# The end of a fused attention and feed-forward kernel, tile by tile instead of stage by stage

## The reference

```python
x = L0_attn_Z_in
x = x + _layernorm(_L0_attn_ref(_layernorm(x), A_l, r_l, B_l, C_l))
x = x + _layernorm(_L0_ffn_ref(_layernorm(x), gate_w, up_w, down_w, gate_s, up_s, down_s))

# _L0_ffn_ref, for xf = x.reshape(b * s, h); h = 2048, inter = 5632
g = jnp.einsum('th,ih->ti', xf, gate_w) * gate_s
u = jnp.einsum('th,ih->ti', xf, up_w) * up_s
hdn = jax.nn.silu(g) * u
out = jnp.einsum('ti,hi->th', hdn, down_w) * down_s
```

## Time and profile before

| what | value |
|---|---|
| median of three runs | 1383.64 us (1381.90 to 1505.44) |
| the profiled execution's own time | 1382.18 us |
| its span on the slowest core, core 3 | 1380.6 us |
| spans of the eight cores | 1372.5 to 1380.6 us |
| granted TensorE clock, mean of each core | 0.928 to 0.930 |
| bytes moved by DMA on core 3 | 104.44 MB |

### The profile page before, as it was taken

The page is one execution under the profiler, slowest core; times in us unless marked ns, Lnnn a source line. Parts: engine busy times, 40 slices in busy tenths (PEclk is TensorE's granted clock), DMA queues, the critical chain, the costliest instruction groups (busy, mean ns, idle before and its releaser), DMA issues.

```text
span 1380.6 us, 12731 instructions; the slowest of 8 cores (1372.5 to 1380.6 us)
## 1 busy us (share of the span) xinstructions
PE 1142.6 (83%) x5236; PEld 505.5 (37%) x5236; DVE 350.3 (25%) x398; ACT 200.9 (15%) x255; POOL 53.7 (4%) x76
## 2 busy tenths in 40 slices
PE   2429889860799999999999999999999999999500
PEld 0103334320444444444444444444444444444200
DVE  2057344357310122101320113110131001312810
ACT  2402333243300000000000000000000000000242
POOL 1000000000000000000000000000000000000000
PEclk9959999985699999999999999999999999999755
DMA  6770000006993513844047440665307633030059
GB/s 116 204 161 1 1 1 0 1 24 240 160 156 63 90 32 47 136 87 88 10 70 127 86 84 1 89 125 92 61 1 116 122 68 61 0 61 0 0 92 151
DMA packets 27592, 104.44 MB, mean 76 GB/s; under 512 B 2320, under 2 KB 4880, under 8 KB 24080
## 3 DMA queue, kind: packets, MB, share of 16 engines
q0 software_dynamic: 23936, 83.63, 36.3%
q1 hardware_dynamic: 2448, 16.81, 3.3%
q10 hardware_dynamic: 1152, 3.20, 0.9%
HBM read 162.09 MB, written 16.78 MB: 130 GB/s over the span
## 4 chain that ended last, share of the span: by engine, by line
PE 66%; DMA 2%; DVE 2%; ACT 1%; issue 1%; POOLq 0%; DVEq 0%; ACTq 0%
PE ps_f L739 22%; PE ps_f L791 22%; PE ps_f L755 22%; DMA y<-w2b 2%; DVE acc L815 1%; ACT w2b L849 1%; DVE hdn L769 1%; DVE acc L804 0%; ACT w2b L820 0%; ACT L833 0%; POOLq L77 0%; DVEq L88 0%; ACT rW L835 0%; ACT tstat L833 0%; ACTq L88 0%
## 5 line engine op out<-in xcount | busy, mean ns | idle before, releaser
L739 PE MATMUL ps_f<-lnfT,gw_sb 128*128 128x512 bf16 x1408 | 313.4, 381 | 5.3 <-PEq L77 5.3
L791 PE MATMUL ps_f<-dwb,hdn 128*128 128x512 bf16 x1408 | 304.9, 379 | 11.4 <-DVE hdn L769 11.4
L755 PE MATMUL ps_f<-lnfT,uw_sb 128*128 128x512 bf16 x1408 | 311.1, 379 | 0.0
L791 PEld LDWEIGHTS ps_f<-dwb,hdn 128*128 128x128 bf16 x1408 | 137.4, 98 | 178.9 <-issue 14.1
L739 PEld LDWEIGHTS ps_f<-lnfT,gw_sb 128*128 128x128 bf16 x1408 | 138.3, 98 | 173.2 <-issue 8.7
L755 PEld LDWEIGHTS ps_f<-lnfT,uw_sb 128*128 128x128 bf16 x1408 | 137.7, 98 | 166.2
L769 DVE SCALAR_TENSOR_TENSOR hdn<-ps_f,us_sb,sg 128x1024 bf16<-128x1024 f32 x44 | 56.5, 1284 | 555.3 <-PE ps_f L755 555.3
L765 ACT ACTIVATE sg<-ps_f,gs_sb 128x1024 bf16<-128x1024 f32 x44 | 49.0, 1114 | 831.3 <-PE ps_f L739 831.3
L426 PE MATMUL ps_t<-att,xTb 128*128 128x512 bf16 x512 | 116.0, 384 | 37.7 <-DMA xTb<-xT 37.7
L804 DVE TENSOR_TENSOR acc<-acc,ps_f 128x2048 f32<-128x2048 f32 x40 | 91.5, 2288 | 172.1 <-PE ps_f L791 172.1
L426 PEld LDWEIGHTS ps_t<-att,xTb 128*128 128x128 bf16 x512 | 49.9, 99 | 100.6 <-issue 43.2
(11 more groups left out here) (103 smaller groups left out, 343.5 us busy)
## 6 DMA issues: line engine op xcount, KB each, us to landing
gw_sb<-gw POOLq DMA_DIRECT2D x22, 1024.0 KB, 8.3
uw_sb<-uw POOLq DMA_DIRECT2D x22, 1024.0 KB, 8.7
dwb<-dw POOLq DMA_DIRECT2D x11, 2048.0 KB, 19.4
xbuf<-x SPq DMA_DIRECT2D x8, 1024.0 KB, 22.6
y<-xbuf SPq DMA_DIRECT2D x8, 1024.0 KB, 4.0
y<-w2b POOLq DMA_DIRECT2D x8, 1024.0 KB, 10.1
xTb<-xT POOLq DMA_DIRECT2D x4, 1024.0 KB, 45.0
xtop_sb<-xtop ACTq DMA_DIRECT2D x2, 1024.0 KB, 9.9
```

The costliest lines, as they stand in the source:

```text
L739: e.matmul(ps_f[:, half, :], gw_sb[:, slot, ht * P:(ht + 1) * P], lnfT[:, ht, half * 512:(half + 1) * 512], start=(ht == 0), stop=(ht == H ...
L755: e.matmul(ps_f[:, 2 + half, :], uw_sb[:, slot, ht * P:(ht + 1) * P], lnfT[:, ht, half * 512:(half + 1) * 512], start=(ht == 0), stop=(ht ...
L791: e.matmul(ps_f[:, bs + hc, :], hdn[:, li, tt * P:(tt + 1) * P], dwb[:, li, hc * 512:(hc + 1) * 512], start=(li == 0), stop=(li == blk - 1)),
```

## The change

The three stages at the end become a function, emit_finale(tt), that is called for each tile of the last group right behind the tile's add. So the end is done tile by tile, in the order DSEQ, in between the down-projection adds. The statistics are computed on one column per tile (t1c, t2c, with rW8[:, 0:1] as scratch), and Ln writes lnt. The Square of a tile now waits for the store of tile tt - 2, since it writes the same buffer of w2b; Identity no longer needs to. What is computed, and the eight stores, stay as they were. The second wait of SP behind the last block was never emitted and is gone.

```diff
+    out_dma = {}
+
+    def emit_finale(tt):
+        pl.vop(lambda e, tt=tt: e.scalar_tensor_tensor(
+            acc[:, tt, :], acc[:, tt, :], 1.0, dsB[:, :], ALU.mult, ALU.mult,
+            accum_out=wsum[:, tt:tt + 1]),
+            w=[("sDV", accadd[(len(BLKS) - 1, tt)])])
+        w1v = pl.v("sDV")
+        pl.aop(lambda e, tt=tt: e.activation(
+            w2b[:, tt % 2, :], acc[:, tt, :], AF.Square,
+            accum_out=wsq[:, tt:tt + 1]),
+            w=[("sDV", w1v)] + ([out_dma[tt - 2]] if tt - 2 in out_dma
+                                else []))
+        sqv = pl.v("sAC")
+        pl.vop(lambda e, tt=tt: e.tensor_scalar(
+            t1c[:, :], wsum[:, tt:tt + 1], 1.0 / D, None, ALU.mult),
+            w=[("sAC", sqv)])
+        pl.vop(lambda e, tt=tt: e.tensor_scalar(
+            t2c[:, :], wsq[:, tt:tt + 1], 1.0 / D, None, ALU.mult))
+        pl.vop(lambda e: e.tensor_tensor(rW8[:, 0:1], t1c[:, :], t1c[:, :],
+                                         ALU.mult))
+        pl.vop(lambda e: e.tensor_tensor(t2c[:, :], t2c[:, :], rW8[:, 0:1],
+                                         ALU.subtract))
+        vst = pl.v("sDV")
+        pl.aop(lambda e, tt=tt: e.activation(
+            lnt[:, tt:tt + 1], t2c[:, :], AF.Ln, bias=c_eps),
+            w=[("sDV", vst)])
+        pl.aop(lambda e, tt=tt: e.activation(
+            rW8[:, tt:tt + 1], lnt[:, tt:tt + 1], AF.Exp, scale=c_nh))
+        rwv = pl.v("sAC")
+        pl.vop(lambda e, tt=tt: e.tensor_tensor(
+            ngW8[:, tt:tt + 1], t1c[:, :], rW8[:, tt:tt + 1], ALU.mult),
+            w=[("sAC", rwv)])
...
+        ngv = pl.v("sDV")
+        pl.aop(lambda e, tt=tt: e.activation(
+            w2b[:, tt % 2, :], acc[:, tt, :], AF.Identity,
+            scale=rW8[:, tt:tt + 1], bias=ngW8[:, tt:tt + 1]),
+            w=[("sDV", ngv)])
+        w2v = pl.v("sAC")
+        osem = "sOUT" if tt % 2 == 0 else "sRL"
+        pl.dma(osem, "gpsimd", t_y.ap()[tt * P:(tt + 1) * P, :],
+               w2b[:, tt % 2, :], w=[("sAC", w2v), ("sSP", SP)], accum=True)
+        out_dma[tt] = (osem, pl.v(osem))
...
             accadd[(bi, tt)] = pl.v("sDV")
+            if bi == len(BLKS) - 1:
+                emit_finale(tt)
```

More of the change, by code:

```diff
@@ L707, in build_nc @@
     dn_prev = {0: None, 4: None}
+    out_dma = {}
[30 more added lines that the diff above has]
+            w=[("sAC", rwv)])
+        pl.vop(lambda e, tt=tt: e.tensor_scalar_mul(
+            ngW8[:, tt:tt + 1], ngW8[:, tt:tt + 1], -1.0))
+        pl.vop(lambda e, tt=tt: e.tensor_tensor(
+            ngW8[:, tt:tt + 1], ngW8[:, tt:tt + 1], ngN8[:, tt:tt + 1],
+            ALU.add))
+        ngv = pl.v("sDV")
[8 more added lines that the diff above has]
+        out_dma[tt] = (osem, pl.v(osem))
@@ L809, in build_nc @@
             accadd[(bi, tt)] = pl.v("sDV")
[L811 to L855, removed]
@@ L856, in build_nc @@
-    pl.em("sync", fn=None, w=[out_dma[-1], out_dma[-2]])
+            if bi == len(BLKS) - 1:
+                emit_finale(tt)
+    pl.em("sync", fn=None, w=[out_dma[6], out_dma[7]])
     pl.emit(nc, sems)
@@ L861, in build_nc @@
     sTl.close()
-    pl.em("sync", fn=None, w=[("sOUT", out_dma[-1])])
     s2.close()
```

## The result

| | before | changed |
|---|---|---|
| median | 1382.48 us (1381.05 at lowest, 10 runs) | 1364.19 us (1362.58 at lowest, 9 runs) |
| ratio, 95% interval | | 0.988, 0.9847 to 0.9913 |
| the profiled execution's own time | 1382.18 us | 1363.61 us |
| span of the slowest core | 1380.6 us (core 3) | 1362.1 us (core 1) |
| first add of the last group to the end of the span | 110.14 us | 91.59 us |

The change makes the kernel 1.2% faster by the ratio, and the medians are 18.3 us apart. The forecast was 1365 us and 17.9 us. In the terms of the forecast this is "within 2%".

The account below looks back on a forecast made before the run. It took two serial end stages, VectorE/ScalarE work then DMA-bound stores, as the bound. Load 1.29, steps 68.95, issue 12.52 and landing 9.5 sum to 92.26 us against 110.14: -17.9 us, forecast 1365 us; eight in ten, 1358 to 1372.

Parts of the forecast that it names:

- within 2%: Whole kernel: a measured time neither faster nor slower than before by over 2%; chance 0.96.
- load of tables: First tile of the last block: one ScalarE table load between Square and Ln delays everything behind it, 1.29 us.
- seven steps: Last block: seven add-to-add steps on VectorE, 68.95 us together.
- add to issue of the store: Last block: a tile's store is issued 12.52 us after its add started.
- last issue to the end of the span: End of the kernel: the last store lands 9.5 us after issue, against 10.66 us before.
- The step: Last block: one tile's chain over VectorE and ScalarE until VectorE's next add, 9.85 us, small operations at 0.17 us.
- tables reloaded per tile: Rival, last block: 14 more table loads around Ln, 18.0 us, giving 1383 us; chance 0.05.
- No wait for a store: Square's wait for the store of two tiles back costs nothing while landing takes under 12.03 us.
- L: Time from a store's issue to its landing; 9.6 to 12.4 us before, lower half expected after.
- TensorE has room: Last block: a tile's 3.45 us of matmuls fit into the 9.85 us step, so TensorE's waiting costs nothing.
- Store issue beside the scaling: Rival: store issue overlaps the next tile's scaling; if scaling must wait, +5.9 us, 1371 us; chance 0.08.
- A DMA-bound tail before, a chain of waits after: Kernel's end: the store tail bound by DMA becomes a latency-bound chain over VectorE and ScalarE; DMA share 0.88 to near 0.6.

Follow-up runs that it names:

- 6: Skewed order: changed kernel with the next tile's add and scaling ahead of this tile's statistics on VectorE, Square writing to sg; 1349.73 us, ratio 0.9785.
- 3: Changed kernel plus one unused 128x1 Silu per tile on ScalarE between Exp and Identity; 1384.04 us, ratio 1.0028.
- 4: Changed kernel plus one unused 128x1 Square per tile on ScalarE between Exp and Identity; 1364.62 us, ratio 0.9892.
- 9: Kernel before the change, but Identity writes into acc in place and stores go out from acc, without buffer waits; 1380.10 us, ratio 1.0.
- 7: Scalar chain: changed kernel with VectorE making mean and Ln bias beside Square, ScalarE doing the rest in a row, Square to sg; 1337.27 us, ratio 0.9693.
- 1: Changed kernel with Square writing to sg, and Identity instead of Square waiting for the store of two tiles back; 1361.64 us, ratio 0.987.
- 2: Changed kernel with one buffer of w2b instead of two, each Square waiting for the store just before it; 1406.12 us, ratio 1.0193.
- 5: Kernel before the change with only scaling and Square moved into the last group's loop, statistics and stores staying behind; 1373.62 us, ratio 0.9953.
- 8: Kernel of 7, but Identity writes into acc in place and stores go out from acc, without buffer waits; 1337.29 us, ratio 0.969.

## Why the prediction was right

Its terms against the changed kernel's core 1:

| term | forecast | measured |
|---|---|---|
| load of tables | 1.29 | 1.29 (first two adds 11.04 us apart, the next 9.75) |
| seven steps | 68.95 | 68.89: adds from 1270.51 to 1340.69 are 70.18, less 1.29 |
| add to issue of the store | 12.52 | 12.48 (1340.69 to 1353.17) |
| last issue to the end of the span | 9.5 | 8.93 (1353.17 to 1362.1) |
| sum | 92.26 | 91.59 |

- *The step.* The 9.85 us were 9.75 to 9.81 in six steps of seven. The small operations take 0.15 to 0.16 us on one column instead of 0.17, so 0.17 was the right end of the range to stand near. One step was 10.18 us, which the forecast did not have (last section). That the seven steps came out at 68.89 against 68.95 is in part luck: this one step made up for the 0.05 us or so by which each of the others was shorter than forecast. The moved order (6) shows by intervention that it is the chain of waits.
- *One table load.* Right, and its price was measured (3, 4). The rival of tables reloaded per tile is out.
- *No wait for a store.* Right: L came out at 7.8 to 8.3 us on the slowest core and at most 9.2 on any other, under the limit of 12.03. The reason given, that stores further apart land sooner, holds for this pair: 8.0 us at 9.8 us apart, 10.1 at 6.4. It goes no further: at 7.5 us apart (6) the median is 7.8, at 16.0 (one buffer) 8.1. My 9.5 for the last landing was 0.6 too long.
- *TensorE has room.* Right: it waits for VectorE five times, 22.9 us in all, and is waited for once, before the first add (4.2 us).
- *Store issue beside the scaling.* This rival is out. In the timeline above the issue at 1284.31 lies within the scaling of 1283.94; they take 0.90 and 2.29 us, what they took apart.
- *A DMA-bound tail before, a chain of waits after.* The last sentence of the sum is borne out by 9 (freeing the buffers of the old kernel gains nothing) and 6 (reordering the new one gains 12 us more).

Of the 41 us by which the first store comes earlier, 24 are given back since stores come every 9.8 us. Taking the chain apart (7) gains 24 us more than the change, until the DMA share is at 1.00.

## What to carry to other kernels

When a staged tail is turned into a loop over tiles, add up one tile's chain over all engines that it visits, with each hop. That sum, not the busiest engine, is the new step if the next tile's first operation stands behind the last hop in an in-order queue; put it ahead of the hops, or keep the statistics on one engine. And before adding buffers for a store that somebody waits for, look at the DMA share: in the old kernel, at 0.88, and in the scalar chain, at 1.00, taking the wait away only moved it into the landing time.

## What the runs showed beyond that

One step of the changed kernel is 0.4 us longer than the others. VectorE sits idle for 0.48 us between two of its own small operations:

```profile
1327.79 0.15 DVE L722 TENSOR_SCALAR t1c<-wsum 128x1 f32<-128x1 f32 x1 [2.38 <-ACT w2b L716]
1328.41 0.15 DVE L725 TENSOR_SCALAR t2c<-wsq 128x1 f32<-128x1 f32 x1 [0.48 <-DVE t1c L722]
```

All eight cores have it at this very instruction of the sixth tile, and nowhere else in the last group. No semaphore comes between the two but VectorE's own. The other traces say more. Counted from the first add of the last group, it stands ahead of VectorE's 49th operation. The kernels of experiments 1 to 4 have it ahead of the 49th too, though it falls there anywhere from 1322 to 1359 us. The skewed order has another operation in that place, and the gap stands ahead of it, on all eight cores:

```profile
1315.76 2.29 DVE L714 SCALAR_TENSOR_TENSOR acc<-acc,dsB 128x2048 f32<-128x2048 f32 x1 [0.46 <-DVE acc L861]
```

Kernels whose VectorE has only 23 operations there (before, 5, 9) or 40 (7, 8) don't have it. So it goes with the place in VectorE's list and not with the data, the tile, the time or the kind of operation. What happens at that place is not shown.

A landing time is not a property of a store: the same 1 MB took 8.0 us at 9.8 us apart, 10.1 at 6.4 and up to 39.2 when eight were issued within 15.2 us. From 7.5 to 16.0 us apart the medians in these traces are all 7.8 to 8.7 us.
